# Attention values of 96 and 64 columns, copied out once and spread by DMA, with regrouped maxima and a reordered SP queue

## The reference, cut to what matters

```python
def _L0_cond_ref(x, mask, Wq, Wo):            # x (16, 512, 1024), mask (16, 1024), 8 heads of 64
    xt = jnp.transpose(x, (0, 2, 1))
    q = xt @ Wq.T
    qh = q.reshape(B, T, NH, dk).transpose(0, 2, 1, 3)
    scores = scale * jnp.einsum('bhqd,bhkd->bhqk', qh, qh)
    logits = (scores * cmask + (1.0 - cmask) * NEG) * rmask
    attn = jax.nn.softmax(logits, axis=-1)
    ctx = jnp.einsum('bhqk,bhkd->bhqd', attn, qh)
    out = ctx.transpose(0, 2, 1, 3).reshape(B, T, D) @ Wo.T
    return jnp.transpose(out, (0, 2, 1))

x = x + _L0_cond_ref(x, cond_2048, L0_cond_Wq, L0_cond_Wo)
x = x + _L1_cond_ref(x, cond_2048[:, None, :], L1_cond_b)   # a causal depthwise convolution, as matmuls
```

## Time and profile before

| | |
|---|---|
| three runs, median (lowest to highest) | 4283.91 us (4280.56 to 4286.85) |
| the profiled execution: its own time | 4281.65 us |
| its span, first to last instruction | 4279.9 us |
| mean granted clock of TensorE | 0.993 |
| PE busy | 4128.9 us, 96% |
| ACT, POOL, DVE busy | 67%, 61%, 58% |

### The profile page before, as it was taken

One profiled execution on the slowest core, in us unless ns is written; L12 is line 12 of the kernel. 1 busy time (PEld: TensorE's weight loads), 2 busy tenths in 40 slices (PEclk: granted clock), 3 DMA queues, 4 the chain that ended last, 5 costly groups with the idle time before them and its releaser, 6 DMA issues. The chain is left out here.

```text
span 4279.9 us, 56952 instructions
## 1 busy us (share of the span) xinstructions
PE 4128.9 (96%) x18688; PEld 2721.4 (64%) x18688; DVE 2491.4 (58%) x2260; ACT 2849.9 (67%) x3905; POOL 2595.8 (61%) x1044
## 2 busy tenths in 40 slices
PE   7999999999999999999999999999999999999799
PEld 4665666666566666656666665666666566666598
DVE  4664555556455655655565565656556565656576
ACT  4775767667576766757676675767667575767465
POOL 4775757667575766757576675757667575766300
PEclk8999999999999999999999999999999999999899
DMA  3323333232333333233333323333332332332488
GB/s 104 82 67 71 80 82 94 71 88 65 74 80 79 94 74 85 65 77 80 77 94 75 84 69 76 81 74 94 75 84 70 74 83 71 94 74 60 128 285 268
DMA packets 286191, 385.34 MB, mean 90 GB/s; under 512 B 148947, under 2 KB 217171, under 8 KB 285782
## 3 DMA queue, kind: packets, MB, share of 16 engines
q1 hardware_dynamic: 285910, 381.57, 34.9%
HBM read 112.28 MB, written 67.11 MB: 42 GB/s over the span
## 5 line engine op out<-in xcount | busy, mean ns | idle before, releaser
L699 POOL TENSOR_TENSOR plo<-p,phi 128x1024 fp32r<-128x1024 f32 x1024 | 2590.4, 2541 | 1404.1 <-ACT phi L629 1399.2
L743 DVE TENSOR_REDUCE mrow<-misc 128x1 f32<-128x1024 f32 x1024 | 1214.0, 1217 | 1067.5 <-PE misc L471 1067.5
L627 ACT ACTIVATE p<-sc 128x512 f32<-128x512 f32 x2048 | 1110.0, 594 | 855.2 <-PE sc L510 610.0
L523 PE MATMUL pv<-phi,val 128*128 128x512 f32 x4096 | 1192.3, 413 | 44.0 <-issue 44.0
L629 ACT ACTIVATE phi<-p 128x1024 fp32r<-128x1024 f32 x1024 | 1086.4, 1061 | 32.5
L523 PEld LDWEIGHTS pv<-phi,val 128*128 128x128 f32 x4096 | 724.1, 188 | 372.4 <-issue 226.0
L509 PE MATMUL sc<-quer,keys 128*128 128x512 f32 x2048 | 917.2, 448 | 23.5 <-issue 18.4
L510 PE MATMUL sc<-quer,keys 96*128 96x512 f32 x2048 | 808.6, 395 | 0.0
L527 PE MATMUL pv<-plo,val 128*128 128x512 f32 x2048 | 644.2, 395 | 0.7 <-POOL plo L699 0.7
L509 PEld LDWEIGHTS sc<-quer,keys 128*128 128x128 f32 x2048 | 386.7, 189 | 195.1 <-issue 75.7
L773 DVE RECIPROCAL den<-den 128x128 f32<-128x128 f32 x512 | 468.4, 935 | 50.2 <-ACT den L616 23.9
(11 more groups left out here) (67 smaller groups left out, 2647.7 us busy)
## 6 DMA issues: line engine op xcount, KB each, us to landing
keys<-hi SPq DMA_DIRECT2D x256, 256.0 KB, 3.1
quer<-mhi SPq DMA_DIRECT2D x256, 256.0 KB, 4.4
keys<-lo SPq DMA_DIRECT2D x128, 256.0 KB, 4.9
quer<-mlo SPq DMA_DIRECT2D x128, 256.0 KB, 3.8
xo<-x SPq DMA_DIRECT2D x64, 512.0 KB, 4.0
x<-xo SPq DMA_DIRECT2D x64, 512.0 KB, 5.1
xin<-x SPq DMA_DIRECT2D x16, 2048.0 KB, 13.6
out<-stage SPq DMA_DIRECT2D x64, 512.0 KB, 6.4
```

Of the source, the lines that this page charges most:

```text
L523: pe.matmul(pv[:, half(h)], val[:, i, t, part, :], phi[:, t % NPHI, half(h)], start=(t == 0 and part == 0), stop=False)
L627: act.activation(p32[:, t % NP32, half(h)], sc[:, h, :], ACT.Exp, scale=SCALE).then_inc(s_p32, 1)
L699: pool.tensor_tensor(plo[:, t % NPLO, :], p32[:, t % NP32, :], phi[:, t % NPHI, :].bitcast(F32), ALU.subtract).then_inc(s_plo, 1)
L743: reduced = dve.tensor_reduce(mrow[:, q:q + 1], misc[:, k, :], AX.X, ALU.max)
```

## The change

`val` becomes 96 columns wide: 64 of values and 32 of ones, in this order for both heads. The matmuls with the high part have 96 columns, those with the low part use the 64 columns of values alone; `pv` is used in partitions 0 to 95 (0 to 63 context, 64 to 95 denominators) for both heads. One activation copies all 96 to a new tile `pvs` in SBUF and raises `s_cab`. The SP queue gets `context_rows`: it waits for `s_cab` and issues three DMAs that write `ca` (64 rows) and `den` (twice the same 32 rows); they raise `s_ctx`, for which the next copy and the reciprocals wait. The last head of all is copied straight from PSUM in halves (`last_context`). In SP's order the load of `xo` part 2 goes from before `operands` to behind it in head (1, 0), and the store of part 1 from the start of head (1, 1) to before `rows` of head (1, 0). The maxima stand at steps 0, 1, 3 and 4, two tiles each, and none at step 2.

```diff
-MAX_AT = {0: [0, 1], 1: [2, 3], 2: [4], 3: [5], 4: [6, 7]}
+ONES = 32
+VC = DK + ONES
+MAX_AT = {0: [0, 1], 1: [2, 3], 3: [4, 5], 4: [6, 7]}
...
-        val = sb("val", [P, 2, KT, 2, P], F32R)
+        val = sb("val", [P, 2, KT, 2, VC], F32R)
+        pvs = sb("pvs", [VC, T], F32)
...
+        CTX = 16 * (1 + DK // ONES)
...
+            def context_rows(b, p, i):
+                sp.wait_ge(s_cab, head(b, p, i) + 1)
+                at = DK * i
+                sp.dma_start(ca[at:at + DK, p % 2, :], pvs[0:DK, :]).then_inc(s_ctx, 16)
+                for r in range(DK // ONES):
+                    sp.dma_start(den[at + r * ONES:at + (r + 1) * ONES, p % 2, :], pvs[DK:VC, :]).then_inc(s_ctx, 16)
...
                         if phase != "first" and (p, i) == (1, 0):
                             store_xo(b - 1, 0)
-                            load_xo(b - 1, 2, True)
                         if phase != "first" and (p, i) == (1, 1):
-                            store_xo(b - 1, 1)
                             load_xo(b - 1, 3, True)
+                        if not (phase == "first" and p == 0 and i == 0):
+                            context_rows(*head_before(b, p, i))
                         if phase != "last" and (p, i) == (2, 1):
                             load_x(b + 1, pair(b, 3) + 1)
                         if i == 0 and not end:
                             operands(*next_pair(b, p))
+                        if phase != "first" and (p, i) == (1, 0):
+                            load_xo(b - 1, 2, True)
+                            store_xo(b - 1, 1)
                         if not (end and i == 1):
                             rows(nb, np_, ni)
...
                 for h in range(2):
-                    for part in range(2):
-                        pe.matmul(pv[:, half(h)], val[:, i, t, part, :], phi[:, t % NPHI, half(h)],
-                                  start=(t == 0 and part == 0), stop=False)
+                    pe.matmul(pv[0:VC, half(h)], val[:, i, t, 0, :], phi[:, t % NPHI, half(h)],
+                              start=(t == 0), stop=False)
+                    pe.matmul(pv[0:DK, half(h)], val[:, i, t, 1, 0:DK], phi[:, t % NPHI, half(h)],
+                              start=False, stop=False)
                 pe.wait_ge(s_plo, n + 1)
                 for h in range(2):
-                    last = pe.matmul(pv[:, half(h)], val[:, i, t, 0, :], plo[:, t % NPLO, half(h)],
+                    last = pe.matmul(pv[0:VC, half(h)], val[:, i, t, 0, :], plo[:, t % NPLO, half(h)],
                                      start=False, stop=(t == KT - 1))
...
                 act.wait_ge(s_pv, (head(b, p, i) + 1) * KT)
+                if not (isinstance(b, int) and b == 0 and p == 0 and i == 0):
+                    act.wait_ge(s_ctx, CTX * head(b, p, i))
...
-                act.activation(ca[mine, p % 2, :], pv[mine, :], ACT.Copy)
-                act.activation(den[mine, p % 2, :], pv[other, :], ACT.Copy).then_inc(s_cab, 1)
+                act.activation(pvs[:], pv[0:VC, :], ACT.Copy).then_inc(s_cab, 1)
+
+            def last_context(h):
+                if h == 0:
+                    act.wait_ge(s_pv, KT * NH * B)
+                at, p = DK, (PAIRS - 1) % 2
+                act.activation(ca[at:P, p, half(h)], pv[0:DK, half(h)], ACT.Copy)
+                for r in range(DK // ONES):
+                    done = act.activation(den[at + r * ONES:at + (r + 1) * ONES, p, half(h)], pv[DK:VC, half(h)], ACT.Copy)
+                done.then_inc(s_cab, 1)
...
             def reciprocals(b, p, part):
                 if part == 0:
-                    dve.wait_ge(s_cab, head(b, p, 1) + 1)
+                    dve.wait_ge(s_ctx, CTX * (head(b, p, 1) + 1))
```

More of the change, by code:

```diff
@@ L253, in build_attention @@
         s_cab = sem("s_cab")
+        s_ctx = sem("s_ctx")
         s_rden = sem("s_rden")
@@ L469, in maxima @@
                 for h in range(2):
-                    rows = slice(DK * h, DK * h + DK)
-                    last = pe.matmul(out[:, half(h)], quer[rows, k, tok(q)], quer[rows, k, half(h)], start=True, stop=True)
+                    mine = slice(DK * h, DK * h + DK)
+                    last = pe.matmul(out[:, half(h)], quer[mine, k, tok(q)], quer[mine, k, half(h)], start=True, stop=True)
                 last.then_inc(full, 1)
@@ L546, in start @@
                 pe.wait_ge(s_ident, 3)
-                pe.wait_ge(s_ones, 4)
+                pe.wait_ge(s_ones, 2)
                 do("start", 0, 0, "head", PHASES["start"]["head"], (0, 0, 0))
@@ L602, in values @@
                     act.wait_ge(s_pv, (head(*nxt) - 1) * KT)
-                at = DK * nxt[2]
-                act.activation(val[:, nxt[2], :, :, at:at + DK],
+                act.activation(val[:, nxt[2], :, :, 0:DK],
                                misc[:, k, :].rearrange("p (k c d) -> p k c d", c=2, d=DK), ACT.Copy).then_inc(s_val, 1)
@@ L611, in copy_context @@
                 act.wait_ge(s_pv, (head(b, p, i) + 1) * KT)
+                if not (isinstance(b, int) and b == 0 and p == 0 and i == 0):
+                    act.wait_ge(s_ctx, CTX * head(b, p, i))
                 if i == 0 and not (isinstance(b, int) and b == 0 and p < 2):
                     act.wait_ge(s_cnorm, pair(b, p) - 1)
-                mine, other = slice(DK * i, DK * i + DK), slice(DK - DK * i, P - DK * i)
-                act.activation(ca[mine, p % 2, :], pv[mine, :], ACT.Copy)
-                act.activation(den[mine, p % 2, :], pv[other, :], ACT.Copy).then_inc(s_cab, 1)
+                act.activation(pvs[:], pv[0:VC, :], ACT.Copy).then_inc(s_cab, 1)
[7 more added lines that the diff above has]
+                done.then_inc(s_cab, 1)
             def exponentials(b, p, i, t, first):
@@ L652, in end @@
             def end():
-                copy_context(B - 1, PAIRS - 1, 1)
+                for h in range(2):
+                    last_context(h)
             run(act, start, batch, end)
@@ L668, in constants @@
                 for i in range(2):
-                    fill = slice(DK - DK * i, P - DK * i)
-                    pool.memset(val[:, i, :, 0, fill].bitcast(F32), 1.0).then_inc(s_ones, 1)
-                    pool.memset(val[:, i, :, 1, fill].bitcast(F32), 0.0).then_inc(s_ones, 1)
+                    pool.memset(val[:, i, :, 0, DK:VC].bitcast(F32), 1.0).then_inc(s_ones, 1)
             def masks():
@@ L770, in reciprocals, with last_reciprocals @@
                 if part == 0:
-                    dve.wait_ge(s_cab, head(b, p, 1) + 1)
+                    dve.wait_ge(s_ctx, CTX * (head(b, p, 1) + 1))
                 d = den[:, p % 2, tok(part)]
+                dve.reciprocal(d, d).then_inc(s_rden, 1)
+            def last_reciprocals(part):
+                d = den[:, (PAIRS - 1) % 2, tok(part)]
                 dve.reciprocal(d, d).then_inc(s_rden, 1)
@@ L861, in end @@
                 for h, done in enumerate((s_half, s_cnorm)):
+                    dve.wait_ge(s_cab, NH * B + h)
+                    if h == 0:
+                        dve.wait_ge(s_ctx, CTX * (NH * B - 1))
                     for part in range(h * KT // 2, (h + 1) * KT // 2):
-                        reciprocals(B - 1, p, part)
+                        last_reciprocals(part)
                     dve.wait_ge(s_rden, KT * pair(B - 1, p) + (h + 1) * KT // 2)
```

## The result

| | before | after |
|---|---|---|
| median (lowest to highest), four runs each on the same chip | 4283.86 us (4280.56 to 4286.85) | 4175.06 us (4170.45 to 4176.01) |
| ratio, 95% interval | | 0.9745 [0.9732, 0.9757] |
| the profiled execution, its span | 4281.65, 4279.9 us | 4174.45, 4172.7 us |

The time fell by 108.8 us. The forecast was 4200 with a range of 4160 to 4262: the sign and the range held, the gain was 25 us larger than the 83 of the sum.

The account below looks back on a forecast made before the run. PE, busy 96% of the span, was taken to bound the kernel. Per batch 3 x 0.80 + 3 x 0.61 + 0.38 + 0.58 = 5.19 us, 83.3 with the end, gave 4200 us, range 4160 to 4262.

Parts of the forecast that it names:

- part 3: Narrower value operands in six context matmuls a step: the weight load is hidden, so the gain is 0.
- The upper end (41 us): Most that narrower value operands could gain, in proportion to columns left out: 0.04 us a step, 41 us in all.
- Part 1: Step 2 of heads (0, 1), (2, 1), (3, 1): one copy for two shortens it from 3.81 to 2.78 us.
- Part 2: Maxima in four groups: -0.38 us a head where PE sets the pace, -0.61 in heads (0, 0), (2, 0), (3, 0).
- Part 4: Three added DMAs a head and SP's new order: all covered, 0; if a cover goes, 16 to 30 us.
- Rival 1: Heads i = 0: POOL's next subtraction precedes `mlo`, PE waits 1.05 us for row maxima; 50 us lost, 4250; chance 0.20.
- Rival 2: The narrower weight loads of the context matmuls do pay: 41 us more gain, 4160; chance 0.10.
- Rival 3: Context matmuls: each change between 96 and 64 columns costs 0.19 us, 778 us in all, 4980; chance 0.10.

Follow-up runs that it names:

- full width run: The changed kernel with operands of 128 columns for all six context matmuls: 4199.81 us, ratio 0.9813 to the kernel before.
- the two runs: The changed kernel with the `xo` load and store at their old SP places, 4175.31 us; the changed kernel with `context_rows` DMAs issued twice, 4176.87 us.
- fastest kernel: The changed kernel with maxima at steps 0, 1, 2, 4 in heads (0, 1), (2, 1), (3, 1) and `mlo` behind step 4's maxima: 4133.66 us.

## Why the prediction was right, and where it was not

**The step that failed is part 3, "So the load is hidden and a shorter one gives nothing: I take 0."** The full width run measures that term at 24.7 us between the medians, and its steps show 20 or somewhat more. Without it the sum was close: 83.3 booked, 82.6 measured (4282.4 to 4199.8). But that agreement is in part luck. The sum takes 5.19 for all 16 batches. The loop's gave 4.90 by the means: 5.4 by the medians, less what four falls of the clock cost. Batches 0 and 15 gave 8.6 and 8.1. Batch 0 has no output projections, so its head (1, 1) gives 0.86 like the other heads i = 1. Its heads (1, 0), (2, 0) and (3, 0) give 0.97 to 0.99, since PE had waited at their step 4 before the change (4.47 where the loop has 3.19), and head (0, 0) gives 2.3, most of it at step 0. The row used for the zero was the transpose with 8 columns, whose load runs under the matmul ahead of it. That is true of the places it resembles, and there the load is hidden to 0.003 us. It says nothing of the places where the load is not hidden: behind the 64-row matmuls of a group, and behind a wait of PE. A better row was in the trace of the kernel before, in PEld behind the group of step 4 of the head of the earlier trace rows:

```profile
1947.07 0.77 PEld L523 LDWEIGHTS pv<-phi,val 128*128 128x128 f32 x4 [0.37 <-issue]
```

The load engine is idle for 0.37 and then loads at the matmul's own start, and from this matmul to the next it was 0.338 (median), where others had 0.231. The upper end (41 us) held, and with it the range. The Trainium skill ("TensorE: Matmul & The Clock Gate", LDWEIGHTS) puts a load at columns/1.2 ns, from which I estimate 27 ns less for 96 columns and 53 for 64. The traces' mean loads are 189, 161 and 136 ns for 128, 96 and 64 columns, so 28 and 53 less: the differences agree, the lengths don't, since by that rule 128 columns would be 107 ns. The 0.029 measured behind a group is near the 28; what decides is where a load is exposed.

**Part 1, one copy.** The mechanism held: one copy, PE 0.10 behind its end, and the run with a second copy brings the wait back. The size was off twice. I set the end of the new copy at the start of the old second one, but ACT starts its next instruction 0.10 before the recorded end of the one ahead; step 2 gave 0.95 at the narrow and 0.89 at full width instead of 1.03. On the other side step 0 of these heads gave 0.13 that was not booked and that goes with the groups. The two cancel: -0.79 in head (2, 1) at full width, -0.80 booked. The number was right by this luck.

**Part 2, the groups.** In the loop's heads i = 0: -0.61 booked, -0.61 measured in (2, 0), both alone and in the full width run. Step 7 went from 2.62 to 2.40, and ACT's wait for POOL at step 5 is gone, ACT waits for PE there. Head (1, 0) gave 0.64 at full width where 0.58 was booked, head (1, 1) 0.44 where 0.38 was. Of the 0.80 booked for heads (0, 1), (2, 1) and (3, 1), however, no share belongs to the groups: with the single copy and the old groups head (2, 1) is just as short (23.21), because the tile at step 2 lay inside the wait.

**Part 4, DMAs and SP.** Zero, and the two runs bear it out. The three DMAs of a head have all landed 4.1 us after the first is issued (median), below the 5 to 8 estimated, since they overlap (3.1 and 3.2 us each).

**Rival 1** did not come about in the loop, by the margin the prediction named: `mlo` asks 0.08 ahead of POOL. In six heads of batches 0 and 15, where POOL is 0.04 to 0.08 ahead, it did: PE waits 0.94 at the transpose and step 5 is 1.07 longer, 6.4 us in all. The prediction read one batch for all sixteen. And it is real in the loop: half a microsecond on DVE ahead of `mlo` costs 59 us. The Trainium skill ("SBUF — State Buffer", Terms) calls the port pair of DVE and GpSimd an exclusive lock for the whole instruction; 3.40 for POOL behind `mlo`, 3.44 and 2.97 for `mlo` behind POOL agree. **Rival 2** is what happened on top of the forecast, by 20 to 25 of its 41 us. **Rival 3** is refuted by the run with a low part of 96 columns. The Trainium skill ("TensorEngine Tiling (Array Packing)", Key Properties) has the engine drain on a change of tiling mode. The 0.38 of a group agrees with that for the change between 128 and 64 rows; between 96 and 64 columns no cost shows, and whether these two count as different modes is open.

**Still open:** what PE waits for at the loop's return (1.2 to 1.6 us idle before, 1.2 to 1.9 after), and why the clock falls behind that wait in some batches and not in others.

## What to carry to other kernels

A cost read at one place holds for places with the same neighbours; before a term is set to zero, read start to start at each different neighbour of the changed instruction, above all behind a change of the array's rows and behind a wait. Look at the first and the last pass of a loop too: a race that the loop's batches win by 0.08 us was lost in both of them. Where an engine waits anyway, work put into the wait is nearly free (a group cost 0.28 there and 0.84 elsewhere) and work taken out of it brings nothing: here the maxima belonged at step 2 of the heads i = 1, not away from it. And count the users of each buffer in a step before a group is moved there.

## What the runs showed of the hardware that was not expected

- Behind 64-row matmuls the weight load of the first 128-row matmul is not overlapped: the time from it to the next matmul was 0.336 us with 128 columns and 0.307 with 96, where others are 0.231. Behind a wait of PE it was 0.307 and 0.282.
- When DVE's multiplication and POOL's subtraction start within 0.1 us of each other, the one recorded first runs at its own length and the other takes longer, by nearly that length: POOL 0.04 ahead, `mlo` 3.44 instead of 1.22; `mlo` 0.06 ahead, POOL 3.40 instead of 2.39. Only right behind a memset on DVE was it otherwise.
- The parts of a change can give more together than alone (109 us against 98), when one part frees an engine whose backlog swallowed the gain of the other.
- TensorE's granted clock fell behind a short idle time. In the fastest kernel PE stood still for 1.86 us before head (0, 0) of batch 8; the stretches around it, in the view of windows (us, busy times by engine, PEclk as a share of 2.4 GHz):

```profile
1935.70:1940.10 4.40, 2.57 (x13) 1.58 (x11) 1.01 (x1) 3.17 (x4) 3.52 (x2) 1.00 0.44 96
1940.50:1943.70 3.20, 3.20 (x10) 1.60 (x9) 0.85 (x1) 0.96 (x2) 1.69 (x1) 0.50 0.09 22
1944.00:1948.00 4.00, 4.00 (x14) 2.03 (x12) 1.21 (x2) 0.92 (x1) 2.35 (x1) 1.00 0.00 0
```

  The clock was at its lower level of 1.2 GHz for a time and then back at 2.4, and the score matmuls stood 0.42 apart instead of 0.23. So a wait there can cost more than its own length: step 0 of the head takes 7.78 where it takes 6.28 without the fall, 1.5 us. The length of the wait alone doesn't decide it. Of the 13 returns of the loop in this kernel the clock fell in seven, behind 1.29 to 2.19 us of idle time, and kept its level in six, behind 1.18 to 1.87. In the change it fell in two (1.91 and 1.67), in the kernel before in none (1.20 to 1.63).
